# A decoder layer with a mixture of experts on one core: the experts' fp32 products become three 16-bit products each, with the weights read at a register's address

## The reference, cut to what matters

```python
h = layernorm(x + o, g1, b1)
probs = softmax(h @ wg); topv, topi = top_k(probs, 2)
w = (topv / topv.sum(-1))[..., None] * one_hot(topi, 8)
h1 = gelu(einsum('bsd,edf->ebsf', h, w1) + bb1)     # 8 experts, d 128, f 512
y = einsum('ebsf,efd->ebsd', h1, w2) + bb2
out = layernorm(h + einsum('ebsd,bse->bsd', y, w))
```

## Time and profile before

| | |
|---|---|
| median of 3 runs | 1290.16 us (1288.4 to 1293.84) |
| profiled execution, its own time | 1299.05 us |
| its span | 1297.8 us |
| mean granted TensorE clock | 0.893 of full speed |
| PE busy | 1063.3 us, 82% |
| POOL busy | 911.1 us, 70% |
| DVE busy | 865.0 us, 67% |
| ACT busy | 824.6 us, 64% |

### The profile page before, as it was taken

One profiled execution on the slowest core, in us unless ns is written; L12 is line 12 of the kernel. 1 busy time (PEld: TensorE's weight loads), 2 busy tenths in 40 slices (PEclk: granted clock), 3 DMA queues, 4 the chain that ended last, 5 costly groups with the idle time before them and its releaser, 6 DMA issues.

```text
span 1297.8 us, 45997 instructions
## 1 busy us (share of the span) xinstructions
PE 1063.3 (82%) x17677; PEld 761.5 (59%) x17677; DVE 865.0 (67%) x2370; ACT 824.6 (64%) x1884; POOL 911.1 (70%) x859
## 2 busy tenths in 40 slices
PE   5888888788998888888988888847788799999552
PEld 2555555554555555555555555637777789999310
DVE  4677776766888777777767776545454466666485
ACT  2355554678999887777777776414445466666377
POOL 3788888866766657777777776766666656667596
PEclk9999898987999999989888997657889999999886
DMA  5465332221233223222222221111212233332453
GB/s 158 129 185 147 88 86 63 63 60 54 75 85 85 80 66 85 68 67 68 79 65 65 77 77 35 52 34 43 61 54 63 66 88 98 99 100 78 143 164 97
DMA packets 132181, 108.61 MB, mean 84 GB/s; under 512 B 19563, under 2 KB 122476, under 8 KB 131932
## 3 DMA queue, kind: packets, MB, share of 16 engines
q1 hardware_dynamic: 123548, 88.29, 24.9%
q0 software_dynamic: 8416, 17.38, 3.8%
HBM read 41.58 MB, written 26.75 MB: 53 GB/s over the span
## 4 chain that ended last, share of the span: by engine, by line
PE 42%; issue 14%; DVE 14%; POOL 14%; ACT 10%; DMA 3%; another core or an unknown queue 2%; DVEq 1%; SPq 1%; POOLq 0%; ACTq 0%
PE bank L1211 7%; PE bank L1202 7%; POOL Plo L769 7%; PE bank L547 3%; PE bank L612 3%; PE bank L550 3%; DVE P L841 2%; DMA xrow<-block_rows 2%; PE bank L487 2%; DVE st L873 2%; DVE mx L817 2%; PE bank L450 2%; PE bank L517 2%; PE bank L510 2%
## 5 line engine op out<-in xcount | busy, mean ns | idle before, releaser
L769 POOL TENSOR_TENSOR Plo<-P 128x1024 f16<-128x1024 f32 x192 | 364.7, 1901 | 162.2 <-ACT P L726 136.1
L1254 POOL DMA_INDIRECT expert_rows<-yo,ix x135 | 173.0, 1281 | 103.3 <-DVE ix L1248 73.4
L1225 ACT ACTIVATE G<-bank,we 128x128 f32<-128x128 f32 x540 | 154.9, 372 | 103.6 <-PE bank L1202 85.3
L817 DVE TENSOR_REDUCE mx<-bank 128x16 f16<-128x1024 f32 x128 | 156.7, 1225 | 42.3 <-PE bank L465 33.2
L687 ACT ACTIVATE Kz<-kh,col 128x512 f16<-128x512 f16 x256 | 167.1, 717 | 0.1
L1211 PE MATMUL bank<-we,G 128*128 128x128 f32 x1080 | 151.5, 286 | 16.7 <-ACT G L1225 12.6
L787 POOL DMA_INDIRECT block_rows<-xs,slots x128 | 132.6, 1036 | 39.8 <-issue 38.4
L510 PE MATMUL bank<-Vh,P 64*128 64x17 f16 (+1 forms) x3072 | 148.6, 170 | 10.2 <-issue 10.2
L726 ACT ACTIVATE P<-bank 128x1024 f32<-128x1024 f32 x128 | 131.1, 1024 | 39.7 <-PE bank L487 38.2
L510 PEld LDWEIGHTS bank<-Vh,P 64*128 64x128 bf16 x3072 | 125.6, 94 | 49.8 <-issue 37.2
L511 PE MATMUL bank<-Vh,Plo 64*128 64x17 f16 (+1 forms) x3072 | 145.9, 168 | 9.4 <-issue 9.3
(11 more groups left out here) (187 smaller groups left out, 2169.5 us busy)
## 6 DMA issues: line engine op xcount, KB each, us to landing
Qz<-qh SPq DMA_DIRECT2D x192, 64.0 KB, 2.0
Kst<-kh SPq DMA_DIRECT2D x192, 64.0 KB
xrow<-block_rows SPq DMA_DIRECT2D x135, 65.0 KB
y_t<-expert_rows SPq DMA_DIRECT2D x16, 512.0 KB, 4.1
Qz<-ql SPq DMA_DIRECT2D x96, 64.0 KB, 2.0
Kst<-kl SPq DMA_DIRECT2D x96, 64.0 KB
xT<-xt SPq DMA_DIRECT2D x16, 256.0 KB, 3.1
xs<-x SPq DMA_DIRECT2D x16, 256.0 KB, 4.1
```

The costliest lines, as they stand in the source:

```text
L769: pool.tensor_tensor(Plo[n % 3][:, :], P32[n % 3][:, :], upper(n), ALU.subtract).then_inc(f_Pl.of(n), 1)
L817: dve.tensor_reduce(columns, bank[:, S_BANK:S_BANK + 2, :].rearrange("p r (j i k) -> p r j i k", i=2, k=S), AX_X, ALU.max, negate=True).th ...
L1225: i = act.activation(G[b][:, c, :], bank[:, 2 + p, c * P:(c + 1) * P], ACT.Gelu_apprx_tanh, bias=we[b][:, B1 + c:B1 + c + 1])
L1254: pool.indirect_dma_start(ydst[:, :], bass.IndirectOffsetOnAxis(ix2[s % 4][:, :], 0), yo[s % 4][:, :], None).then_inc(b_sc.of(s), 16)
```

## The change

**The products.** Each fp32 factor is written as a high 16-bit part and a low 16-bit part (the difference). A product becomes three 16-bit products: high x high, high x low, low x high. So each of the eight fp32 products of a block becomes three.

**The weights.** They are split once. In the stream, SP loads 16 chunks of 128 x 512 fp32 into the old `gate` tiles, ACT writes the high part to `wx` (fp16) and POOL the low part. The two bias loads and nine weight loads of `mixture` are gone.

**The copy and the address.** DVE no longer copies weights. PE itself loads the block's expert from `expert_of` into a register, and reads `wx` at an address worked out from it.

**The activations.** ACT writes `xhi` (fp16) in place of `hTb` and DVE writes `xlo`. The high part of `G` is the upper half of each fp32 number, read in place with a stride, and DVE writes the low part `Glo` (128 x 512).

**The rows and biases.** There are eight buffers `xrow` in place of four. The block's biases come by a DMA of their own into eight buffers `eb`, for which SP loads the expert into a register too.

```diff
@@ tiles
-    WW = 2 * F_N + FC + P
-    W1, W2, B1, B2 = 0, F_N, 2 * F_N, 2 * F_N + FC
+    W1, W2, HIGH, LOW = 0, 2, 0, 1
-    wx = sb("wx", [P, E_N, WW])
+    wx = sb("wx", [P, E_N, 4, F_N], F16)
@@ the list mixture loses the two bias loads and the nine loads of w1 and w2
...
@@ new, in the attention stream
+    CHUNKS = 2 * E_N
+    w_ld = count("w_ld", 16, len(gate))
+    w_high, w_low = count("w_high"), count("w_low")
+    LOADED, HIGHS, LOWS = {}, {}, {}
+    for j in range(0, CHUNKS, 2):
+        g = AT["self", 1] + j
+        for c in range(2):
+            LOADED.setdefault(GT * (g - 1), []).append(j + c)
+            HIGHS[GT * g + c] = j + c
+        LOWS[GT * (g + 1) + 3] = j
+        LOWS[GT * (g + 2) + 1] = j + 1
+
+    def expert_part(j, part):
+        return wx[:, j // 2, (W1, W2)[j % 2] + part, :]
+
+    def sp_expert_weights(j):
+        e = j // 2
+        sp.wait_ge(*f_OTg(NG - 1))
+        sp.wait_ge(*w_low(j - len(gate)))
+        if j % 2 == 0:
+            sp.dma_start(gate[j % len(gate)][:, :], w1[e]).then_inc(w_ld.of(j), 16)
+        else:
+            sp.dma_start(gate[j % len(gate)][:, :].rearrange("f (c d) -> f c d", d=P),
+                         w2[e].rearrange("(c f) d -> f c d", f=P)).then_inc(w_ld.of(j), 16)
+
+    def act_expert_weights(j):
+        act.wait_ge(*w_ld(j))
+        act.copy(expert_part(j, HIGH), gate[j % len(gate)][:, :]).then_inc(w_high.of(j), 1)
+
+    def pool_expert_weights(j):
+        pool.wait_ge(*w_high(j))
+        pool.tensor_tensor(expert_part(j, LOW), gate[j % len(gate)][:, :], expert_part(j, HIGH), ALU.subtract).then_inc(w_low.of(j), 1)
 
@@ sp_slot, act_slot, pool_slot (the last two at the end of a slot)
+        for j in LOADED.get(s, ()):
+            sp_expert_weights(j)
+        if s in HIGHS:
+            act_expert_weights(HIGHS[s])
+        if s in LOWS:
+            pool_expert_weights(LOWS[s])
@@ moe_phase
-        xrow = [sb(f"xrow{p}", [P, RW]) for p in range(4)]
+        AHEAD = 8
+        xrow = [sb(f"xrow{p}", [P, RW]) for p in range(AHEAD)]
-        we = [sb(f"we{p}", [P, WW]) for p in range(4)]
+        eb = [sb(f"eb{p}", [P, FC + P]) for p in range(AHEAD)]
...
         def sp_expert(s):
             if s == EARLY_BLOCKS:
                 sp.wait_ge(s_table[1], TABLE_DONE[1])
                 for i in range(NG - 2, NG):
                     sp.wait_ge(*l_rows(i))
-            sp.wait_ge(*b_xT(s - 4))
-            sp.wait_ge(*b_ix(s - 4))
+            sp.wait_ge(*b_xT(s - AHEAD))
+            sp.wait_ge(*b_ix(s - AHEAD))
             first = sp.value_load(row_of[0:1, order[s]:order[s] + 1], min_val=0, max_val=(E_N * REGION + SPARE) * P)
-            sp.dma_start(xrow[s % 4][:, :], buf[bass.ds(first, P), :]).then_inc(b_ld.of(s), 16)
+            sp.dma_start(xrow[s % AHEAD][:, :], buf[bass.ds(first, P), :]).then_inc(b_ld.of(s), 16)
+            sp.wait_ge(*b_g(s - AHEAD))
+            sp.wait_ge(*b_yo(s - AHEAD))
+            e = sp.value_load(expert_of[0:1, order[s]:order[s] + 1], min_val=0, max_val=E_N - 1)
+            sp.dma_start(eb[s % AHEAD][:, :], biases[bass.ds(e, 1), :, :].rearrange("o p w -> (o p) w")).then_inc(b_eb.of(s), 16)
+
+        def pe_expert_of(s):
+            if s == EARLY_BLOCKS:
+                pe.wait_ge(s_table[1], TABLE_DONE[1])
+            chosen_of[s] = pe.value_load(expert_of[0:1, order[s]:order[s] + 1], min_val=0, max_val=E_N - 1)
 
         def pe_expert_turn(s):
             pe.wait_ge(*b_ld(s))
-            pe.wait_ge(*b_xTs(s - 2))
-            pe.transpose(bank[:, s % 2, 0:P], xrow[s % 4][:, 0:P], ident[:, :]).then_inc(b_xT.of(s), 1)
+            pe.wait_ge(*b_xlo(s - 2))
+            pe.transpose(bank[:, s % 2, 0:P], xrow[s % AHEAD][:, 0:P], ident[:, :]).then_inc(b_xT.of(s), 1)
+
+        def expert_weights(s, part, c):
+            return wx[:, bass.ds(chosen_of[s], 1), part, c * P:(c + 1) * P].rearrange("p o w -> p (o w)")
 
         def pe_expert_in(s):
-            p, b = s % 2, s % 4
-            pe.wait_ge(*b_xTs(s))
-            pe.wait_ge(*b_we(s))
+            p = s % 2
+            pe.wait_ge(*b_xlo(s))
             pe.wait_ge(*b_g(s - 2))
             for c in range(FC):
-                i = pe.matmul(bank[:, 2 + p, c * P:(c + 1) * P], we[b][:, W1 + c * P:W1 + (c + 1) * P],
-                              hTb[p][:, :], start=True, stop=True)
+                o = bank[:, 2 + p, c * P:(c + 1) * P]
+                pe.matmul(o, expert_weights(s, W1 + HIGH, c), xhi[p][:, :], start=True, stop=False)
+                pe.matmul(o, expert_weights(s, W1 + HIGH, c), xlo[p][:, :], start=False, stop=False)
+                i = pe.matmul(o, expert_weights(s, W1 + LOW, c), xhi[p][:, :], start=False, stop=True)
             i.then_inc(b_z.of(s), 1)
+
+        def high(v):
+            return v[:, :].bitcast(BF16)[:, 1::2]
 
         def pe_expert_out(s):
             p, b = s % 2, s % 4
-            pe.wait_ge(*b_g(s))
+            pe.wait_ge(*b_glo(s))
             pe.wait_ge(*b_yo(s - 2))
+            o = bank[:, 4 + p, 0:P]
             for c in range(FC):
-                i = pe.matmul(bank[:, 4 + p, 0:P], G[b][:, c, :], we[b][:, W2 + c * P:W2 + (c + 1) * P],
-                              start=c == 0, stop=c == FC - 1)
+                cs = slice(c * P, (c + 1) * P)
+                pe.matmul(o, high(G[b])[:, cs], expert_weights(s, W2 + HIGH, c), start=c == 0, stop=False)
+                pe.matmul(o, high(G[b])[:, cs], expert_weights(s, W2 + LOW, c), start=False, stop=False)
+                i = pe.matmul(o, Glo[b][:, cs], expert_weights(s, W2 + HIGH, c), start=False, stop=c == FC - 1)
             i.then_inc(b_y.of(s), 1)
+            del chosen_of[s]
 
         def act_expert_turned(s):
             act.wait_ge(*b_z(s - 2))
             act.wait_ge(*b_xT(s))
-            act.copy(hTb[s % 2][:, :], bank[:, s % 2, 0:P]).then_inc(b_xTs.of(s), 1)
+            act.copy(xhi[s % 2][:, :], bank[:, s % 2, 0:P]).then_inc(b_xhi.of(s), 1)
+
+        def dve_expert_turned(s):
+            dve.wait_ge(*b_z(s - 2))
+            dve.wait_ge(*b_xhi(s))
+            dve.tensor_tensor(xlo[s % 2][:, :], bank[:, s % 2, 0:P], xhi[s % 2][:, :], ALU.subtract).then_inc(b_xlo.of(s), 1)
 
         def act_expert(s):
             p, b = s % 2, s % 4
             act.wait_ge(*b_y(s - 4))
+            act.wait_ge(*b_glo(s - 4))
+            act.wait_ge(*b_eb(s))
             act.wait_ge(*b_z(s))
             for c in range(FC):
-                i = act.activation(G[b][:, c, :], bank[:, 2 + p, c * P:(c + 1) * P], ACT.Gelu_apprx_tanh,
-                                   bias=we[b][:, B1 + c:B1 + c + 1])
+                i = act.activation(G[b][:, c * P:(c + 1) * P], bank[:, 2 + p, c * P:(c + 1) * P], ACT.Gelu_apprx_tanh,
+                                   bias=eb[s % AHEAD][:, c:c + 1])
             i.then_inc(b_g.of(s), 1)
 
-        def dve_expert_weights(s):
-            if s == EARLY_BLOCKS:
-                dve.wait_ge(s_table[1], TABLE_DONE[1])
-            e = dve.value_load(expert_of[0:1, order[s]:order[s] + 1], min_val=0, max_val=E_N - 1)
-            dve.wait_ge(*b_yo(s - 4))
+        def dve_expert_low(s):
+            b = s % 4
             dve.wait_ge(*b_y(s - 4))
-            dve.wait_ge(*b_g(s - 4))
-            dve.tensor_copy(we[s % 4][:, :], wx[:, bass.ds(e, 1), :].rearrange("p o w -> p (o w)")).then_inc(b_we.of(s), 1)
+            dve.wait_ge(*b_g(s))
+            dve.tensor_tensor(Glo[b][:, :], G[b][:, :], high(G[b]), ALU.subtract).then_inc(b_glo.of(s), 1)
 
...
-            dve.tensor_tensor(yo[b][:, :], bank[:, 4 + p, 0:P], we[b][:, B2:B2 + P], ALU.add).then_inc(b_yo.of(s), 1)
+            dve.wait_ge(*b_eb(s))
...
+            dve.tensor_tensor(yo[b][:, :], bank[:, 4 + p, 0:P], eb[s % AHEAD][:, FC:], ALU.add).then_inc(b_yo.of(s), 1)
@@ the loop over steps s
-            if s < NBLK:
-                dve_expert_weights(s)
+            if 2 <= s < NBLK + 2:
+                dve_expert_low(s - 2)
...
                 sp_expert(s)
+                pe_expert_of(s)
                 pe_expert_turn(s)
                 act_expert_turned(s)
+                dve_expert_turned(s)
```

More of the change, by code:

```diff
@@ L1117, in moe_phase @@
         wb = sb("wb", [P, NT])
-        xrow = [sb(f"xrow{p}", [P, RW]) for p in range(4)]
+        AHEAD = 8
+        xrow = [sb(f"xrow{p}", [P, RW]) for p in range(AHEAD)]
         ix2 = [sb(f"ix2_{p}", [P, 1], U32) for p in range(4)]
-        hTb = [sb(f"hTb{p}", [P, P]) for p in range(2)]
-        we = [sb(f"we{p}", [P, WW]) for p in range(4)]
-        G = [sb(f"G{p}", [P, FC, P]) for p in range(4)]
+        xhi, xlo = ([sb(f"{n}{p}", [P, P], F16) for p in range(2)] for n in ("xhi", "xlo"))
+        eb = [sb(f"eb{p}", [P, FC + P]) for p in range(AHEAD)]
+        G = [sb(f"G{p}", [P, FC * P]) for p in range(4)]
+        Glo = [sb(f"Glo{p}", [P, FC * P], F16) for p in range(4)]
         yo = [sb(f"yo{p}", [P, P]) for p in range(4)]
@@ L1246, in dve_expert_rows @@
             dve.wait_ge(*b_sc(s - 4))
```

(4 more changed lines are left out.)

27 lines of the change are left out of this document (11 added, 16 removed).

## The result

| | us | runs |
|---|---|---|
| before | 1289.28 (1282.47 to 1293.84) | 4 |
| after | 1427.68 (1421.24 to 1434.13) | 4 |

What follows compares the result with a forecast made beforehand. The prediction took PE's instruction queue, at 2.7 us a block, as the bound. Late +57, early +21 and stream +4 us made +82 on the profiled 1299 us, 1381; 9 us less for the median gave 1372 us, range 1275 to 1450.

Steps and rivals of the forecast that it cites:

- PE's queue is the bound: Experts' blocks: feeding PE through its queue takes 2.7 us for a block, against 1.89 us before, and sets the pace.
- An address, 0.107 us: PE's queue: each register instruction for an address costs 0.107 us as on DVE, 16 of them 1.7 us a block.
- The load with its test, 0.65 us: PE's queue: loading the expert into a register and testing it costs 0.65 us in each block, as on DVE.
- The step: One block on PE: 2.7 us on its queue, plus 0.1 us kept for stalls.
- Late, +57 us: Late part of the experts' blocks: 80 blocks at 2.7 + 0.1 us in place of 2.09 us, +57 us.
- Early, +21 us: Early part: 55 blocks at 2.7 us and 35 us of the stream's remainder, 184 us against 163, +21 us.
- Stream, +4 us, by less than 10: Stream ahead of the experts: weight splits on ACT and POOL add 4 us, less than 10, as neither is busiest.
- SP, 2.34 us: SP's work on a block's rows and biases doubles to 2.34 us, hidden only behind PE's 2.7 us.
- 1: Rival: an address on PE costs 0.09 us as on SP, a block 2.4 us, 1331 us in all; chance 0.20.
- 2: Rival: an address costs 0.07 us or less, SP decides at 2.34 us, 1277 us in all; chance 0.13.
- 3: Rival: PE's queue is slower than SP's in all things, a step near 4 us or more; chance 0.07.
- 4: Rival: PE's clock falls to half in places, the array needs 2.6 us, up to +20 us; no chance of its own.

Runs made afterwards that it cites:

- e2: The changed kernel with PE reading expert 0's weights at fixed addresses, without register load, test or address instructions on PE: 1.0384 times the kernel before.
- e5: The changed kernel with e1's slots and W2's two halves paired in one product, 12 addresses per block in place of 16: 1.0484 times the kernel before.
- e9: The kernel before, unchanged, measured again with a profile of its own: 1.0025 times the kernel before.
- e10: The changed kernel, unchanged, measured again with a profile of its own: 1.1058 times the kernel before.
- e1: The changed kernel with the first of each pair of POOL's low parts of the weight split one slot later: 1.0858 times the kernel before.
- e8: The changed kernel with e1's slots, PE's register load and test kept, but all products at expert 0's fixed address: 1.0279 times the kernel before.

## Why the prediction came out as it did

- *PE's queue is the bound* (the term "that decides"): right, and shown. e2 took the register work away and the step fell to SP's pace, 2.33 us in the median and 2.47 in the mean; e5 took four addresses away and it fell by 0.51. The signs that were named came: the "issue" idle time ahead of PE's groups, the load of 0.66 us, ACT, DVE and POOL waiting in a row.
- *An address, 0.107 us*: mis-sized. It was 0.124 from the spacing and 0.128 by e5. The instruction's length, 46 ns, lies between SP's 42 and DVE's 57. The prediction priced an address up to the start of what uses it, and that gap was as priced, 49 ns. What it left out is the time from there to the next address instruction, 29 ns in which the weight load is passed on, so that the whole gap is 78 ns. It makes 16 x 0.017 = 0.27 us a step. The Trainium skill (Advanced Engine Details and Errata, Clock Domains) gives PE's sequencer the rate of SP's. The 46 ns are near SP's 42, as it would have it. The 0.09 us that the prediction drew from it for a whole address is further from the measurement than 0.107 is.
- *The load with its test, 0.65 us*: 0.66. *Three waits, 0.3*: 0.39, with the dispatch of the transposition. *Feeding the pairs, nothing*: nothing; the pair without an address comes 15 ns behind the other.
- *The step*, 2.7 on the queue and 2.8 with stalls: 3.09. *Late, +57 us*: +82.5. 80 x (3.09 - 2.80) = 23 us of the 25 missing are the step's, most of it the address.
- *Early, +21 us*: +15 in after, +27 between e9 and e10. That the sum came right is luck in part. At 3.09 us a block, 55 blocks take 170 us and not 149, so that only 10 us (after) or 25 us (e10) were left for the stream's remainder, for which 35 were priced. The two errors have opposite signs.
- *Stream, +4 us, by less than 10*: wrong. It was +30, and +23 between e9 and e10. The step that failed is "neither is the busiest engine there", which prices added work by idle shares. What happened wasn't the 24 us of added work, which cost nothing in e1 (858.1 us), but a slower rhythm in which all engines do less. Its cause stays open.
- *SP, 2.34 us*: 2.33, the median step in e2 and e8, where PE waits for rows. *`Glo` 0.69, `xlo` 0.29*: 0.69 and 0.29. *POOL 1.37*: 0.96, less than priced, and hidden either way.
- *Removed loads, nothing*: no run tested it alone.
- The rivals: 1 (an address at 0.09 and a step of 2.4) and 2 (0.07 and less) fell by the price of an address. 3 (0.05 us for each matmul with a register) fell too, by the pair that comes 15 ns apart. 4: the clock was 1.00 in the late part, so it had no part there. It was 0.92 in the early part of after and 0.85 in that of e10, which took 14 us longer.

Late +82.5, early +15 and stream +23 to the first block make the 120 us up to the last block. The other 2 us to the difference of the spans, 122, lie behind it. The rest up to the 138 us between the medians is that the profiled execution of before lies 10 us above its median and that of after 6 us below. Against the forecast of 1372 us 56 us are missing. 40 of them lie in the profiled executions: 25 late, 19 in the stream and 2 behind the last block, less the 6 that the early part stayed below its term. The other 16 come from where these executions lie among the others.

## What to carry to other kernels

Before a copy into a fixed buffer is replaced by register addresses on PE, count the addresses: here each cost 0.124 us of PE's queue, a load of the register 0.37 us and its test 0.29, and twelve of them already took up what the cheaper 16-bit products gave back to the array. Where a choice must stay, make a product wide, so that one address serves more columns. Change one thing at a time: of this bundle the eight row buffers were worth 0.7%, and the rest hid it.

Where engines run in lockstep, one profile of each kernel doesn't price a small addition to them: look at several executions, of both kernels on the same chip, and at the clock of the next stage, before an explanation is believed. Here a give-back that two pairs of profiles suggested was gone in the third.
